# The last batch of a decoder layer taken apart: maxima spread by matmuls, inner rows turned on TensorE, two products and three row halves moved to VectorE

## The chip, the cores and the metric

The kernel runs on one core of a Trainium2 chip. The metric is the time of one execution on the device in microseconds (us); lower is better.

## The reference

One decoder layer over 16 batches of 256 rows by 256 features, float32, post-norm:

```
x = layernorm(x + attention(x))            # 16 heads of 16, bias -8*|i-j|/512, softmax
x = layernorm(x + mlstm(x, ctx, ctx))      # 4 heads of 64
x = layernorm(x + ffn(x))                  # BitLinear 256 -> 1024 -> 256, SiLU gate

mlstm, per head:  a = igate - cumsum(log_sigmoid(fgate)); m = running max of a
                  D[s,t] = exp(a[t] - m[s]) for t <= s;  C = (q k^T / 8) * D
                  h = C v / (max(|sum C|, exp(-max_log_D)) + 1e-6)
                  out = norm over the 64 features of a head, times outnorm_scale
ffn:              act_quant: scale = 127/max|row|, round to integers
                  h = silu(gate) * up;  y = act_quant(h) @ ternary(w_down)^T
```

## The kernel before, in words

The 256 rows of a batch are TT = 2 tiles of 128 partitions (index t), so most tiles are [128, 2, 256]; the inner rows `h` and `hq` of the feed-forward part are [128, 2, 1024]. Each engine has one written-out order of calls: `opening()` for the first batches, `body(b)` for batches 4 to 11 and `closing()` for the rest. The engines meet only at semaphores, and each executes its list strictly in order. Batches are overlapped: while the 16 heads of attention of batch b are computed, the mLSTM part of b-1 and the feed-forward part of b-2 run between them, so after the last attention head of batch 15 there remain its mLSTM part, the feed-forward parts of batches 14 and 15 and little else.

PSUM has eight banks: two for scores (`pS`), two for transposed scores (`pT`), one for attention outputs (`pO`), and three (`pA`, `pB`, `pC`) that all other products lease in the order in which TensorE's list asks for them. A lease waits until the product three leases back has been read.

The steps that matter here, for batch c (mLSTM) or f (feed-forward):

- Layer norms 0, 1 and 2 share one scheme. VectorE takes statistics (`row_stats`, L2786; `row_moments`, L2795) and adds epsilon (`row_eps`, L2805); GpSimd raises to the power -1/2 (`rstd`, L1411); VectorE makes the shift (`row_shift`, L2816), which waits for GpSimd; ScalarE writes both row tiles for norms 0 and 1 (`normed`, L1994), GpSimd for norm 2 (`output`, L1477).
- The gates of the mLSTM part: ScalarE reads them (L1931 to L1955), VectorE sums (`forget_sums`, L3034), GpSimd adds (`input_rows`, L1498), VectorE takes the running maximum `mm` [4, 256] (`running_max`, L3042). SyncE writes `mm` to DRAM (`save_max`, L1246) and reads it back into all 128 partitions (`spread_max`, L1253). ScalarE then exponentiates `mb` (`mem_late`, L1914; `mem_weights`, L1922), GpSimd zeroes the causal part (`mem_causal`, L1506), VectorE multiplies with the scores (`mem_weights`, L3023).
- Head norm: VectorE up to L2908 (`head_norm`), GpSimd multiplies by the norm weights (`mem_scaled`, L1514) and adds the residual (`mem_residual`, L1522), then norm 1.
- Feed-forward: rows rounded (`quantised` L2005, `quantised_rows` L1454), turned (`rows_turned` L275, `rows_copy` L2022), gate and up products in four parts (L395, L410), tanh (L2086), `gated` (L2958), `gated_up` (L2969), row maximum (`inner_max`, L2977), scale factors (L2985 to L3002), rounding on ScalarE (`scaled`, L2094) and GpSimd (`inner_quantised`, L1466), a DMA transpose per tile (`turn_inner`, L1264), the down product (`down`, L457), `ffn_residual` (L3013), norm 2 and `store` (L1269).

The PSUM banks and the few lines that cannot be told otherwise:

```
other, n = leases[-len(shared)]          # three leases back
signal, k = freed[other]
eng.wait_ge(signal.sem, signal.at(n, k))
```

Of the kernel before, what the change touches and what calls it, by code (L numbers as in the profile page):

```python
# [58 lines left out]
def build(nc, x, ctx, Wq, bq, Wk, bk, Wv, bv, Wo, bo, pos_bias, ig_w, ig_b, fg_w, fg_b, norm_w,  # L59
          w_gate, w_up, w_down, out):  # L60
    es = ExitStack()
    with es:
# [58 lines left out]
        emT = sb("emT", [P, 2, TT, XH])  # L121
        cT = sb("cT", [P, 2, 3 * P])
# [82 lines left out]
        o_out = sig("o_out", 16)  # L205

# [10 lines left out]
        leases, banks = [], {}  # L217

# [26 lines left out]

        @block.tensor
        def _(pe):
# [199 lines left out]
            def down(f, t):  # L448
# [6 lines left out]
                pe.wait_ge(hq_in[t].sem, hq_in[t].at(f, 16))  # L455
# [72 lines left out]
            def x1_turned(c, par):  # L528

                if not live(c):  # L530
                    return
                bank = lease(pe, "x1T", c)
                pe.wait_ge(x1_a.sem, x1_a.at(c, TT))
                transposes(bank, x1[:, par, :, :], ident[:], x1T_ps)

# [322 lines left out]
            def closing():  # L858
                turned(11, 15)
                mem_values(10, 0)  # L860
                mem_values(10, 1)
                mem_scores(10, 1)
                values(11, 3, 1)
                mem_values(10, 2)
                heads_turned(11, 0)
                heads_turned(11, 1)
                turned(12, 0)
                scores(12, 6, 0)
                scores(12, 7, 0)
                mem_values(10, 3)  # L870
                attention_turned(11)
                scores(12, 8, 0)
                turned(12, 1)
                turned(12, 2)
                out_proj(11)
                scores(12, 9, 0)
                turned(12, 3)
                ctx_turned(11)
                turned(12, 4)
                down(9, 0)  # L880
                turned(12, 5)
                scores(12, 10, 0)
                v_proj(13)
                x1_turned(11, 1)
                down(9, 1)
                gate_parts(11)
                scores(12, 11, 0)
                x_turned(14, 0)
                gate_sums(11)
                scores(12, 12, 0)  # L890
                values(12, 0, 0)
                k_proj(14)
                scores(12, 13, 0)
                scores(12, 14, 0)
                turned(12, 6)
                turned(12, 7)
                scores(12, 15, 0)
                q_proj(14)
                scores(13, 0, 1)
                rows_turned(10)  # L900
                gate_proj(10, 0)
                scores(13, 1, 1)
                turned(12, 8)
                values(12, 1, 0)
                turned(12, 9)
                turned(12, 10)
                scores(13, 2, 1)
                up_proj(10, 0)
                gate_proj(10, 1)
                exponents_turned(11)  # L910
                scores(13, 3, 1)
                up_proj(10, 1)
                turned(12, 11)
                up_proj(10, 2)
                gate_proj(10, 2)
                turned(12, 12)
                gate_proj(10, 3)
                values(12, 2, 0)
                scores(13, 4, 1)
                turned(12, 13)  # L920
                up_proj(10, 3)
                turned(12, 14)
                mem_scores(11, 0)
                turned(12, 15)
                mem_values(11, 0)
                scores(13, 5, 1)
                turned(13, 0)
                mem_scores(11, 1)
                values(12, 3, 0)
                mem_values(11, 1)  # L930
                scores(13, 6, 1)
                heads_turned(12, 0)
                scores(13, 7, 1)
                heads_turned(12, 1)
                mem_values(11, 2)
                turned(13, 1)
# [3 lines left out]
                out_proj(12)  # L940
                turned(13, 2)
                ctx_turned(12)
                scores(13, 9, 1)
                turned(13, 3)
                turned(13, 4)
                turned(13, 5)
                down(10, 0)
                v_proj(14)
                scores(13, 10, 1)
# [3 lines left out]
                x_turned(15, 1)  # L953
                scores(13, 11, 1)
                gate_sums(12)
                scores(13, 12, 1)
                turned(13, 6)
                values(13, 0, 1)
                scores(13, 13, 1)
                scores(13, 14, 1)  # L960
                q_proj(15)
                turned(13, 7)
                turned(13, 8)
                scores(13, 15, 1)
                k_proj(15)
                scores(14, 0, 0)
                rows_turned(11)
# [3001 lines left out]
```

## Time and profile before

| | us |
|---|---|
| median of 3 executions | 722.99 (721.27 to 723.14) |
| the profiled execution | 722.18 |
| its span, first to last instruction | 720.5 |

| engine | busy us | share of the span |
|---|---|---|
| TensorE (PE) | 622.3 | 86% |
| VectorE (DVE) | 602.0 | 84% |
| ScalarE (ACT) | 566.9 | 79% |
| GpSimd (POOL) | 505.9 | 70% |

The busy shares are averages over the whole execution; the closing part of it is much emptier than the middle. In a row of a timeline stand the start, the duration, the engine, the line, the operation, the tiles written and read with their shapes, and in brackets how long the engine had been idle and which instruction released it. Consecutive instructions of one line are merged (x2, x8).

### The profile page before, as it was taken

The numbers are of one execution on the slowest core, as the hardware profiler recorded it, in microseconds if no ns is written. First come the engines' busy times: TensorE is split into PE (matmuls) and PEld (weight loads), VectorE is DVE, ScalarE is ACT, GpSimd is POOL, SyncE is SP. The second block draws the span as 40 slices with busy tenths as digits, with TensorE's granted clock in tenths as the row PEclk, the third lists the DMA queues.
The fourth block names the chain that finished last, engine by engine and source line by source line (L and its number), as shares of the span: only waits on it lengthen the run. The fifth ranks groups of instructions, "written<-read, shape, count | busy, mean of one in ns | idle before, by whom it ended". The sixth has DMA issues, their size and how long they took to land. (4 is left out here: it accounts for less than half of the span.)

```text
span 720.5 us, 16641 instructions
## 1 busy us (share of the span) xinstructions
PE 622.3 (86%) x4892; PEld 451.7 (63%) x4892; DVE 602.0 (84%) x2387; ACT 566.9 (79%) x1189; POOL 505.9 (70%) x781
## 2 busy tenths in 40 slices
PE   5688998999999999999999999998988978684642
PEld 3465785777767676867686868676665746452311
DVE  2475798999999999999999999998979998685853
ACT  1165979899998989898989898988769687875531
POOL 3185678778897878888888888875968746644432
PEclk9599999999999999999999999999999999898856
DMA  8995939455556575647273737454194611111201
GB/s 237 142 214 119 131 76 137 98 89 123 85 104 103 104 105 101 106 93 114 78 113 83 115 66 132 70 100 79 57 131 82 115 42 46 21 61 37 73 16 44
DMA packets 106104, 69.20 MB, mean 96 GB/s; under 512 B 47200, under 2 KB 106016, under 8 KB 106016
## 3 DMA queue, kind: packets, MB, share of 16 engines
q1 hardware_dynamic: 106016, 68.14, 51.9%
q8 instruction: 41, 0.67, 0.4%
q14 instruction: 47, 0.39, 0.2%
HBM read 28.73 MB, written 4.26 MB: 46 GB/s over the span
## 5 line engine op out<-in xcount | busy, mean ns | idle before, releaser
L2774 DVE CUSTOM_DVE_ANT_0 sc<-pS,bias 128x256 f32<-128x256 f32 x512 | 198.5, 415 | 25.6 <-PE pS L291 18.4
L1444 POOL TENSOR_SCALAR sc<-sc,mx 128x256 f32<-128x256 f32 x336 | 166.5, 506 | 28.1 <-DVE mx L2774 27.0
L1895 ACT ACTIVATE pr<-pT 128x512 f32<-128x512 f32 x256 | 152.2, 614 | 16.4 <-PE pT L309 16.1
L309 PE MATMUL pT<-ident,sc 128*128 128x128 f32 x1024 | 152.9, 276 | 6.8 <-POOL sc L1444 3.8
L309 PEld LDWEIGHTS pT<-ident,sc 128*128 128x128 f32 x1024 | 118.0, 141 | 29.7 <-issue 14.7
L291 PE MATMUL pS<-ks,qs 96*128 96x256 bf16 x512 | 94.0, 275 | 7.8 <-DVE mx L2774 6.8
L1883 ACT ACTIVATE sc<-sc,mx 128x256 f32<-128x256 f32 x176 | 90.8, 528 | 3.5 <-DVE mx L2774 3.5
L291 PEld LDWEIGHTS pS<-ks,qs 96*128 96x128 bf16 x512 | 44.2, 98 | 42.6 <-DVE mx L2774 23.0
L326 PE MATMUL pO<-pr,va 128*32 128x256 f32 x1024 | 68.7, 386 | 0.6 <-ACT oT L1905 0.6
L1411 POOL TENSOR_TENSOR rs<-ve,minus_half 128x2 f32<-128x2 f32 x48 | 37.6, 782 | 33.1 <-DVE ve L2805 33.0
L1466 POOL TENSOR_SCALAR hq<-h 128x512 bf16<-128x512 f32 x64 | 38.5, 618 | 29.0 <-ACT h L2094 27.7
L1994 ACT ACTIVATE x<-y,shift,rs 128x256 f32<-128x256 f32 x64 | 34.9, 594 | 27.9 <-DVE shift L2816 27.6
L1506 POOL TENSOR_SCALAR_AFFINE_SELECT mb<-mb 128x256 f32<-128x256 f32 x64 | 26.0, 408 | 33.8 <-ACT mb L1922 33.6
L2094 ACT ACTIVATE h<-h,magic,hs 128x1024 f32<-128x1024 f32 x32 | 39.6, 1238 | 7.6 <-DVE hs L3002 7.6
L326 PEld LDWEIGHTS pO<-pr,va 128*32 128x32 f32 x1024 | 26.8, 109 | 26.5 <-issue 10.8
L2774 DVE DVE_READ_ACCUMULATOR2_ANT mx<- 128x1 f32 x512 | 41.6, 81 | 0.0
L2786 DVE BATCH_NORM_STATS2 st<-y 128x6 f32<-128x256 f32 x96 | 35.8, 416 | 5.8 <-POOL y L1522 4.3
L2977 DVE TENSOR_REDUCE hs<-h 128x1 f32<-128x1024 f32 x32 | 38.8, 1213 | 0.3
L1422 POOL TENSOR_SCALAR parts<-qk_f 128x512 bf16<-128x512 f32 x31 | 19.5, 629 | 27.7 <-ACT qk_f L2053 27.2
L1424 POOL TENSOR_TENSOR qk_f<-qk_f,parts 128x512 f32<-128x512 f32 x31 | 36.8, 1188 | 2.6
L1434 POOL TENSOR_TENSOR parts<-qk_f,parts 128x512 bf16<-128x512 f32 x31 | 36.1, 1163 | 2.6
L1922 ACT ACTIVATE mb<-mb,aT 128x256 f32<-128x256 f32 x64 | 34.6, 541 | 0.8
(291 smaller groups left out, 1672.9 us busy)
## 6 DMA issues: line engine op xcount, KB each, us to landing
qs<-parts SPq DMA_DIRECT2D x96, 128.0 KB, 4.7
ks<-parts SPq DMA_DIRECT2D x96, 128.0 KB, 4.9
mb<-mrows SPq DMA_DIRECT2D x16, 512.0 KB, 3.8
xin<-in_x SPq DMA_DIRECT2D x16, 256.0 KB, 3.6
xb<-in_x SPq DMA_DIRECT2D x16, 256.0 KB, 5.3
cx<-in_ctx SPq DMA_DIRECT2D x32, 128.0 KB, 2.1
out<-hq SPq DMA_DIRECT2D x16, 256.0 KB, 2.2
bias<-in_L_attn_pos_bias SPq DMA_DIRECT2D x4, 768.0 KB, 9.2
```

The costliest lines, as they stand in the source:

```text
L291: ins = pe.matmul(pS[s % 2][:, t * S:t * S + S], qs[par][:, s, t * P:t * P + P], ks[par][:, s, :], start=True, stop=True)
L309: ins = pe.transpose(bank[:, kt * S + t * P:kt * S + t * P + P], sc[:, s % RING, t, kt * P:kt * P + P], ident[:])
L326: ins = pe.matmul(pO[32 * j:32 * j + 32, 0:S], va[par][:, kt, hd, :], pr[:, hd % RING, kt, :], start=(kt == 0), stop=(kt == TT - 1))
L1411: pool.tensor_tensor(rs[:, which, :], ve[:, which, :], minus_half[:, 0:TT], ALU.pow)\
L1424: pool.tensor_tensor(src, src, parts[:, 0, which, :, :], ALU.subtract).then_inc(split.sem, 1)
L1444: ins = pool.tensor_scalar(sc[:, s % RING, t, :], sc[:, s % RING, t, :], -1.0, mx[:, s % RING, t:t + 1], ALU.mult, ALU.add)
L1466: ins = pool.tensor_scalar(hq[:, t, j * 512:j * 512 + 512], h[:, t, j * 512:j * 512 + 512], 1.0, -MAGIC, ALU.mult, ALU.add)
L1883: act.activation(sc[:, s % RING, 0, :], sc[:, s % RING, 0, :], ACT.Identity, bias=mx[:, s % RING, 0:1], scale=-1.0).then_inc(neg_a.sem, 1)
L1895: act.activation(flat(pr[:, s % RING, :, :]), pT[s % 2][:, :], ACT.Exp, scale=-1.0)\
L2094: act.activation(h[:, t, :], h[:, t, :], ACT.Identity, bias=magic[:, :], scale=hs[:, 4, t:t + 1])\
L2774: dve.tensor_tensor_reduce(out=sc[:, s % RING, t, :], in0=pS[s % 2][:, t * S:t * S + S], in1=bias[:, s, t * P:t * P + S][:, ::-1], scale=1 ...
L2977: dve.tensor_reduce(hs[:, 0, t:t + 1], h[:, t, :], AX.X, ALU.max, apply_absolute_value=True)\
```

## The change

`max_rows_of` makes the last batch read the running maxima from PSUM; `final(batch)` is true for batch 15 alone. For that batch:

- `save_max`, `spread_max` and both `turn_inner` leave SyncE's list. TensorE spreads the maxima by four float32 products with a selector `heads_of` (made once, in VectorE's closing list) into the score banks, and turns the inner rows by sixteen bf16 transposes into the score banks; ScalarE and VectorE copy a half each into `hqT`.
- `mem_scaled` and `mem_residual` move from GpSimd to VectorE.
- In norms 0, 1 and 2 ScalarE (or GpSimd) writes row tile 0 and VectorE row tile 1.
- ScalarE rounds the inner rows in halves of 512 columns, and GpSimd follows half by half.
- All five `closing()` lists are written anew, from batch 12 of attention on; opening and body are the same.

```diff
+        def final(batch):
+            return isinstance(batch, int) and batch == B - 1
+        def max_rows_of(c, hh):
+            return pS[hh // 2][:, hh % 2 * S:hh % 2 * S + S] if final(c) else mb[:, hh, 0:S]
...
# TensorE, down
-                pe.wait_ge(hq_in[t].sem, hq_in[t].at(f, 16))
+                if final(f):
+                    pe.wait_ge(it_a.sem, t + 1)
+                    pe.wait_ge(it_v.sem, t + 1)
+                else:
+                    pe.wait_ge(hq_in[t].sem, hq_in[t].at(f, 16))
...
+            def max_spread(c):
+                pe.wait_ge(mm_v.sem, mm_v.at(c, 1))
+                pe.wait_ge(h_of.sem, 1)
+                pe.wait_ge(s_mx.sem, TT * NH * B)
+                for hh in range(XH):
+                    ins = pe.matmul(pS[hh // 2][:, hh % 2 * S:hh % 2 * S + S], heads_of[:, hh, :], mm[:, :], start=True, stop=True)
+                ins.then_inc(spread.sem, 1)
+
+            def inner_turned(f, t):
+                pe.wait_ge(hq_g.sem, hq_g.at(f, t + 1))
+                pe.wait_ge(d_sb.sem, d_sb.at(f, 2 * XH))
+                for j in range(FT):
+                    bank = (pS, pT)[j // 4][t][:, :].bitcast(BF16)
+                    ins = pe.transpose(bank[:, j % 4 * P:j % 4 * P + P], hq[:, t, j * P:j * P + P], ident_b[:])
+                    if j % 4 == 3:
+                        ins.then_inc(it_ps.sem, 1)
...
# ScalarE, and below it VectorE
+            def inner_copy(f, t):
+                act.wait_ge(it_ps.sem, 2 * t + 1)
+                act.wait_ge(h_v.sem, h_v.at(f, 7))
+                act.activation(flat(hqT[:, t, 0:4, :]), pS[t][:, :].bitcast(BF16)[:, 0:512], ACT.Copy).then_inc(it_a.sem, 1)
...
+                n = 2 if final(f) else 1
+                for j in range(n):
+                    part = h[:, t, j * FI // n:(j + 1) * FI // n]
+                    act.activation(part, part, ACT.Identity, bias=magic[:, :], scale=hs[:, 4, t:t + 1]).then_inc(hr_a.sem, 1)
...
+            def normed_half(batch, which, par):
+                o, y = ((x1[:, par, :, :], y1), (x2, y2))[which]
+                wait(dve, rs_s[which], batch, TT)
+                if which == 1:
+                    wait(dve, y_v, batch - 1, TT)
+                dve.tensor_scalar(o[:, 1, :], y[:, 1, :], rs[:, which, 1:2], shift[:, which, 1:2], ALU.mult, ALU.add)\
+                    .then_inc(half_v[which].sem, 1)
+            def mem_scaled(f):
+                dve.wait_ge(gn_v.sem, gn_v.at(f, 16))
+                dve.tensor_tensor(y2[:], y2[:], nw_bc[:, :].unsqueeze(1).to_broadcast([P, TT, D]), ALU.mult)\
+                    .then_inc(mem_v.sem, 1)
+            def mem_residual(f, par):
+                dve.wait_ge(mem_v.sem, 1)
+                dve.tensor_tensor(y2[:], y2[:], x1[:, par, :, :], ALU.add).then_inc(mem_v.sem, 1)
+            def inner_copy(f, t):
+                dve.wait_ge(it_ps.sem, 2 * t + 2)
+                dve.wait_ge(h_v.sem, h_v.at(f, 7))
+                dve.tensor_copy(hqT[:, t, 4:8, :].rearrange("p j q -> p (j q)"), pT[t][:, :].bitcast(BF16)[:, 0:512]).then_inc(it_v.sem, 1)
+            def output_half(e):
+                wait(dve, rs_s[2], e, TT)
+                wait(dve, o_out, e - 1, 16)
+                dve.tensor_scalar(ot[:, 1, :], y3[:, 1, :], rs[:, 2, 1:2], shift[:, 2, 1:2], ALU.mult, ALU.add)\
+                    .then_inc(out_v.sem, 1)
```

The end of VectorE's new list, with what moved marked (from the last attention output on):

```diff
                 row_shift(15, 0)
+                normed_half(15, 0, 1)
                 ffn_residual(13, 0)
-                ffn_residual(13, 1)
                 row_stats(14, 1)
                 row_moments(14, 1)
+                ffn_residual(13, 1)
                 row_eps(14, 1)
                 row_shift(14, 1)
...
-                row_eps(13, 2)
                 forget_sums(15)
                 running_max(15)
                 max_rows(15)
                 gated(14, 0)
                 gated_up(14, 0)
                 gated(14, 1)
+                gated_up(14, 1)
+                row_eps(13, 2)
                 row_shift(13, 2)
-                gated_up(14, 1)
                 inner_max(14, 0)
...
                 head_norm(15)
-                ffn_residual(14, 0)
+                mem_scaled(15)
+                mem_residual(15, 1)
                 row_stats(15, 1)
                 row_moments(15, 1)
                 row_eps(15, 1)
+                ffn_residual(14, 0)
                 ffn_residual(14, 1)
                 row_shift(15, 1)
-                row_stats(14, 2)
+                normed_half(15, 1, 1)
                 row_max(15)
...
                 inner_factor(15, 1)
+                inner_copy(15, 0)
+                inner_copy(15, 1)
                 ffn_residual(15, 0)
...
                 row_shift(15, 2)
+                output_half(15)
```

And of TensorE's:

```diff
                 down(13, 0)
-                down(13, 1)
                 ctx_turned(15)
                 x1_turned(15, 1)
+                down(13, 1)
                 gate_parts(15)
...
                 gate_proj(14, 2)
+                up_proj(14, 2)
                 gate_proj(14, 3)
-                up_proj(14, 2)
+                max_spread(15)
                 up_proj(14, 3)
                 mem_scores(15, 0)
...
                 gate_proj(15, 0)
+                up_proj(15, 0)
                 gate_proj(15, 1)
-                up_proj(15, 0)
+                gate_proj(15, 2)
                 up_proj(15, 1)
-                gate_proj(15, 2)
                 gate_proj(15, 3)
                 up_proj(15, 2)
                 up_proj(15, 3)
+                inner_turned(15, 0)
+                inner_turned(15, 1)
                 down(15, 0)
                 down(15, 1)
```

On ScalarE `scaled(14, 0)` stands behind `mem_out(15, 0)` instead of ahead of `mem_weights(15, 2)`.

## Rows read from the trace of the kernel before

**Rows 1.** Busy time in three stretches (PE, PEld, DVE, ACT, POOL busy us; clock; DMA).

```profile
400.00:500.00 100.00, 96.27 (x783) 72.62 (x776) 93.33 (x398) 89.20 (x186) 80.17 (x122) 1.00 0.54 93
560.00:600.00 40.00, 32.78 (x276) 23.02 (x275) 37.18 (x146) 32.05 (x67) 25.10 (x41) 1.00 0.35 71
...
700.00:721.00 21.00, 5.81 (x24) 2.60 (x22) 8.50 (x25) 3.74 (x4) 4.20 (x7) 0.66 0.20 50
```

**Rows 2.** The chain that ended last: start, us, what ended it.

```profile
684.50 1.26 POOL y L1514
685.84 1.26 POOL y L1522
...
706.12 1.25 ACT h L2094
707.44 1.20 POOL hq L1466 x2
```

**Rows 3.** VectorE's timeline, 683 to 700 us.

```profile
683.73 0.69 DVE L2908 TENSOR_TENSOR y<-y,nrm 128x512 f32<-128x512 f32 x1 [1.53 <-POOL nrm L1486]
...
687.13 0.75 DVE L2786 BATCH_NORM_STATS2 st<-y 128x6 f32<-128x256 f32 x2 [2.32 <-POOL y L1522]
...
688.33 0.48 DVE L3013 SCALAR_TENSOR_TENSOR y<-pC,hs,x 128x256 f32<-128x256 f32 x1
...
690.74 0.69 DVE L2915 TENSOR_REDUCE fs<-x 128x2 f32<-128x512 f32 x1 [0.50 <-ACT x L1994]
...
699.50 0.69 DVE L2969 TENSOR_TENSOR h<-h,pB 128x512 f32<-128x512 f32 x1
```

**Rows 4.** ScalarE's timeline, 671 to 695 us.

```profile
671.85 0.40 ACT L1914 ACTIVATE mb<-mb,aT 128x128 f32<-128x128 f32 x1 [0.23 <-DMA mb<-mrows]
...
689.61 1.09 ACT L1994 ACTIVATE x<-y,shift,rs 128x256 f32<-128x256 f32 x2 [9.81 <-DVE shift L2816]
...
694.61 0.60 ACT L2022 ACTIVATE xqT<-pA 128x512 bf16<-128x512 bf16 x1 [1.47 <-PE pA L275]
```

**Rows 5.** VectorE's timeline, 657 to 675 us.

```profile
657.36 0.21 DVE L2805 TENSOR_SCALAR ve<-mv 128x1 f32<-128x1 f32 x2
658.39 0.33 DVE L2816 TENSOR_SCALAR shift<-mv,rs 128x1 f32<-128x1 f32 x2 [0.82 <-POOL rs L1411]
...
670.27 1.22 DVE L2977 TENSOR_REDUCE hs<-h 128x1 f32<-128x1024 f32 x1
...
674.41 0.56 DVE L3023 SCALAR_TENSOR_TENSOR cT<-pC,mb 128x384 f32<-128x384 f32 x1
```

**Rows 6.** TensorE's timeline, 648 to 712 us.

```profile
648.50 1.97 PE L370 MATMUL pA<-woT,x1T 128*128 128x256 f32 x8 [0.78 <-ACT x1T L1975]
...
670.29 0.61 PE L395 MATMUL pC<-wg,xqT 128*128 128x512 bf16 x2
...
693.99 0.59 PE L275 MATMUL pA<-ident_b,xq 128*128 128x128 bf16 x4 [8.38 <-POOL xq L1454]
...
697.01 1.06 PE L410 MATMUL pA<-wu,xqT 128*128 128x512 bf16 x2
...
710.04 1.87 PE L457 MATMUL pA<-wd,th 128*128 128x256 bf16 x8 [7.35 <-DMA th<-hq]
```

**Rows 7.** SyncE's timeline: issue time of three transfers.

```profile
666.72 0.27 SPq L1246 DMA_DIRECT2D mrows<-mm  x1
...
706.85 3.05 SPq L1264 DMA_TRANSPOSE th<-hq  x2
717.94 0.38 SPq L1269 DMA_DIRECT2D out<-hq  x1
```

**Rows 8.** The timeline of all engines at the start, 15.9 to 16.4 us.

```profile
15.91 1.40 POOL L1424 TENSOR_TENSOR qk_f<-qk_f,parts 128x512 f32<-128x512 f32 x1
16.34 1.52 DVE L2708 TENSOR_TENSOR qk_f<-qk_f,parts 128x512 f32<-128x512 f32 x1
```

**Rows 9.** GpSimd's timeline, the last instructions.

```profile
716.82 1.09 POOL L1477 TENSOR_SCALAR hq<-y,rs,shift 128x256 f32<-128x256 f32 x2 [0.48 <-DVE shift L2816]
```

More of the change, by code:

```diff
@@ L205, in build @@
         o_out = sig("o_out", 16)
+        h_of, spread, it_ps, it_a, it_v, out_v = (sig(n) for n in ("h_of", "spread", "it_ps", "it_a", "it_v", "out_v"))
+        half_v, mem_v = [sig(f"half_v{i}") for i in range(2)], sig("mem_v")
         freed = {
@@ L1475, in output @@
                 wait(pool, o_out, e - 1, 16)
-                for t in range(TT):
+                for t in range(1 if final(e) else TT):
                     ins = pool.tensor_scalar(ot[:, t, :], y3[:, t, :], rs[:, 2, t:t + 1], shift[:, 2, t:t + 1],
@@ L1992, in normed @@
                     wait(act, y_v, batch - 1, TT)
-                for t in range(TT):
+                for t in range(1 if final(batch) else TT):
                     act.activation(o[:, t, :], y[:, t, :], ACT.Identity, bias=shift[:, which, t:t + 1],
@@ L2501, in closing @@
+                mem_late(12, 0)
+                gate_tanh(11, 2)
+                exponentials(13, 12)
+                negated(13, 14)
+                mem_weights(12, 0)
+                negated(13, 15)
+                mem_late(12, 1)
+                gate_tanh(11, 3)
+                exponentials(13, 13)
+                negated(14, 0)
+                negated(14, 1)
                 mem_weights(12, 1)
                 mem_late(12, 2)
+                negated(14, 3)
+                exponentials(13, 14)
@@ L2783, in row_stats @@
                 y, signal = ((y1, ln1), (y2, ln2), (y3, ln3))[which]
-                wait(dve, *((ln1, batch, 1), (gn_g, batch, 3), (y_v, batch, 2))[which])
+                wait(dve, *((ln1, batch, 1), (mem_v, 2, 0) if final(batch) else (gn_g, batch, 3), (y_v, batch, 2))[which])
                 for t in range(TT):
@@ L3688, in closing @@
+                row_moments(12, 1)
+                ffn_residual(11, 1)
                 biased(14, 9, 0)
+                row_eps(12, 1)
                 biased(14, 9, 1)
-                ffn_residual(11, 1)
-                row_stats(12, 1)
                 row_stats(11, 2)
-                row_moments(12, 1)
-                row_eps(12, 1)
+                row_shift(12, 1)
                 biased(14, 10, 0)
-                row_shift(12, 1)
                 biased(14, 10, 1)
+                row_moments(11, 2)
@@ L3733, in closing @@
-                biased(15, 3, 0)
-                gated(12, 3)
+                gated(12, 3)
+                inner_bound(12, 0)
+                gated_up(12, 3)
+                biased(15, 3, 0)
+                mem_weights(13, 0)
+                row_shift(11, 2)
+                inner_scale(12, 0)
+                mem_weights(13, 1)
+                inner_factor(12, 0)
                 biased(15, 3, 1)
-                inner_scale(12, 0)
+                head_stats(13, 0)
+                inner_max(12, 1)
```

1011 lines of the change are left out of this document (503 added, 508 removed).

## The prediction

> **What bounds the kernel now.** I read the busy time by stretches first, then the chain of waits, then each engine's timeline after 650 us. In the middle TensorE is busy 96.3 of 100 us and VectorE 93.3: nothing there is touched. From 560 to 600 us VectorE has the most work, 37.2 of 40 us, and from 700 us on no engine is busy half the time [rows 1]: a chain of dependent steps sets the pace. The reader should see in the chain that it goes through GpSimd's two passes over y, the last rounding on ScalarE and GpSimd, then the wait for a DMA transpose and two down products [rows 2, 6]. The change works on this chain, and it also writes all closing lists anew, so two questions must be kept apart: what the last batch gains, and what its neighbours pay.
>
> The sum is made on the profiled execution: 722.18 us, a span of 720.5 and 1.7 around it, 0.8 below the median of 722.99.
>
> **Norm product and residual.** On GpSimd they start at 684.50 and 685.84 and take 1.26 each; the statistics start at 687.13 [rows 2, 3]. On VectorE a product of this size with both inputs in SBUF takes 0.69 [rows 3]; two with a hand-over of 0.03 each, from the end of `head_norm` at 684.42, put the statistics at 685.9: **-1.2**. The other end is 1.52, what VectorE took for a 128x512 difference while GpSimd ran a 1.40 us one beside it [rows 8]; twice that would be 687.5, a loss of 0.4. I take 0.69, since GpSimd's own list has nothing between `head_rstd(15)` and `rstd(15, 1)`.
>
> The Trainium skill ("SBUF — State Buffer", Who interferes with whom) says that a VectorE instruction with two SBUF inputs contends with a GpSimd instruction that reads SBUF. The two rows named last agree with it. By that rule alone, with GpSimd busy, this part would lose its gain; it is the last rival below.
>
> **Row halves.** Norm 1: ScalarE writes two tiles in 1.09 from 689.61, and the row maximum starts at 690.74 [rows 3, 4]. One tile is a little over half of it, so the maximum can start at about 690.2. VectorE's half (0.48 for the 256-column `ffn_residual` [rows 3] as the upper end) is done by then: **-0.5**. Norm 0 gives nothing: see below. Output: GpSimd writes two tiles in 1.09 from 716.82 and the store goes out at 717.94 [rows 7, 9]; with one tile each it is half: **-0.5**. Each of these is between 0 (VectorE's half as late as ScalarE's second) and -0.55.
>
> **Inner rows.** ScalarE takes 1.25 for 1024 columns and GpSimd then 1.20 for two halves [rows 2]. In halves GpSimd's last 0.6 follows ScalarE's second half, which ends some 0.3 later than the single pass (a pass of 512 takes 0.60 [rows 4], twice that and overheads about 1.5): -0.3. Then, before, 1.40 us from GpSimd's end at 708.64 to the down product at 710.04 [rows 2, 6]. After: eight transposes, four taking 0.59 at the low clock [rows 6], so about 0.14 to start and 0.9 to run, and the copies of tile 0 (0.60 on ScalarE) are over meanwhile; those of tile 1 end before the first down product does. -0.3. The down products wait behind both `inner_turned`, and stay at 1.87 each: the clock is low there before (0.66 on the mean [rows 1]). Bounds: 0 if the transposes run long, -1.5 if the clock has risen for part of the down products (a 128x512 pair takes 0.61 at 2.4 GHz and 1.06 at 1.2 [rows 6]). Together **-0.6**.
>
> **Maxima by matmuls.** The DMA pair is issued from 666.72 and ScalarE starts on `mb` at 671.85: 5.1 us [rows 4, 7]. The four products have 256 float32 columns each, like the four of L370, which took 1.97 at the high clock [rows 6]. But TensorE's list has them behind `gate_proj(14, 3)`, which was issued at 670.29, so with 0.6 for it and 0.4 for the one now ahead of it they run from 671.3 to 673.2, later than the DMA landed by 1.3. `mem_late`, `mem_weights` and the selection of head 0 need 1.4 more, so VectorE's first product (674.41 before [rows 5]) is not late only because the next part but one delays it anyway: **0**. Bounds: -0.5, and +0.9 if the clock is still low (3.9 for the four).
>
> **What the new lists cost.** Three places can be read in the lists.
> `down(13, 1)` goes behind `x1_turned(15)`, and `ffn_residual(13, 1)` from before the statistics of norm 1 of batch 14 to a place just ahead of its `row_eps`. That `row_eps` is at 657.36, and its chain releases ScalarE, whose list then runs without a gap through the gates. An `ffn_residual` takes 0.48, 0.4 of it until the next starts: **+0.4**. It also buries the half of norm 0, whose product was not the last wait here.
> `row_eps(13, 2)` stood hundreds of nanoseconds ahead of everything in an idle time; now it stands directly before `row_shift(13, 2)`, between `gated_up(14, 1)` and `inner_max(14, 0)`. The shift waits for GpSimd's power: the same pair at 657.36 and 658.39 left VectorE idle for 0.82 [rows 5]. From `inner_max` at 670.27 to 674.41 [rows 5] VectorE has hardly a gap, and the rest of batch 15 hangs on it: eps 0.1 and the wait 0.8, **+0.9**. Zero is the lower end.
> The feed-forward list of batch 15 puts `up_proj(15, 0)` ahead of `gate_proj(15, 1)` and `gate_proj(15, 2)` ahead of `up_proj(15, 1)`. A pair is 0.85 at the low clock. The second tanh then comes 0.85 later, which only just meets VectorE; the second up product ends at 699.8, while its reader started at 699.50 [rows 3]: **+0.3**, between 0 and a whole pair, 0.85.
>
> **The rest of the closing lists,** batches 12 to 15 of attention, some 480 to 650 us. The same work in another order. What I can count: in VectorE's list `row_shift` follows `row_eps` at once three more times and once less, and twice the running maximum follows the forget sums with nothing between (a similar trip through GpSimd). Each is up to 0.8 of idle VectorE, 3.2 net if each is on the path, in a stretch where VectorE has 7% to spare [rows 1]; where TensorE or ScalarE is last it costs nothing. A better packing could give as much. I take **+0.6**, between -3 and +5.
>
> **Sum:** -1.2 -0.5 -0.5 -0.6 +0 +0.4 +0.9 +0.3 +0.6 = **-0.6**: 721.6 for an execution like the profiled one, and 722.4 against the median of 722.99. A measurement of this kernel tells about 0.3%, 2.2 us, from no change, so this is no change.
>
> **The rivals.**
> 1. *The two waits cost nothing* (+0.4 and +0.9 hidden) and the rest is neutral: what is left is -2.8 +0.3 = -2.5, 720.5. For it: ScalarE and TensorE also have work in 656 to 675 us. Against: VectorE's rows there are contiguous.
> 2. *The new lists pack better* before 650 us, by 3: -0.6 -0.6 -3 = -4.2, 718.8. For it: TensorE is busy only 32.8 of 40 us from 560 on [rows 1]. Against: more round trips in VectorE's list.
> 3. *VectorE's in-order waits for GpSimd decide* (slower). It decides once the four net trips fall into 500 to 620 us while GpSimd has other work ahead of the power, so that in every second one the blocking of a two-input operation (1.52 for 0.69, 0.8 more [rows 8]) comes on top of the 0.8: four trips at 1.2 are +4.8 instead of +0.6, in all -1.2 +4.8 = +3.6, 726.6. For it: VectorE at 93% there. Against: the trips are spread over batches with slack on TensorE's side.
> 4. *GpSimd is reading SBUF while VectorE does the moved products*: +0.4 instead of -1.2, in all +1.0, 724.0. Against: its rounding of batch 14 has to end before `head_rstd(15)`.
>
> **How the numbers follow.** Forecast 0.48 (all of it within 0.3%, 720.8 to 725.2), rival 1 0.18 (three quarters of it just beyond 0.3% faster), rival 2 0.14 (faster), rival 3 0.14 (slower), rival 4 0.06 (same, a fifth slower with drift). Faster 0.13 + 0.14 = 0.27; slower 0.14 + 0.04 for the upper edge of the forecast's unknown part = 0.18; within 0.3% 0.55. Range 719.2 to 725.6: it takes in rivals 1 and 4 and part of rivals 2 and 3. The likeliest one's own range is 721.0 to 724.5.
>
> **What would show it.** VectorE's statistics of norm 1 of batch 15 start 1.5 after `head_norm(15)` ends (2.7 before), with 0.69 for each product; the row maximum starts 0.6 after the shift; `down(15, 0)` starts 1.1 after GpSimd's last half; the store is issued 0.6 after GpSimd starts its tile. VectorE is idle 0.8 before `row_shift(13, 2)`. `mem_late(15, 0)` starts at the end of the spreading products and not later than 1.5 before VectorE's first product. Wrong would be: the attention residual of batch 15 (650.5 before) moved by more than 1, which is the rest of the lists; no idle time at `row_shift(13, 2)`; down products at the high clock.

## The result, and the profile after

The changed kernel takes 729.91 us (median of 7 executions, 724.63 to 731.16), the kernel before in the same session 723.14 (720.53 to 725.09). The ratio is 1.0076, 95% interval 1.0045 to 1.0106: slower, beyond the forecast range. (The two medians differ by 6.8 us; by the ratio, in which all executions count, it is 5.5. The table of runs and the sums below go by the ratios.) The profiled execution took 729.92 with a span of 728.1.

Busy time by stretches, the same three as in [rows 1], then three finer ones of the changed kernel (PE, PEld, DVE, ACT, POOL busy us; clock; DMA):

```profile
400.00:500.00 100.00, 94.29 (x776) 71.03 (x779) 92.40 (x393) 87.49 (x185) 79.36 (x119) 1.00 0.59 99
560.00:600.00 40.00, 33.06 (x265) 23.43 (x266) 34.16 (x135) 31.24 (x67) 23.83 (x37) 0.96 0.35 68
700.00:721.00 21.00, 10.76 (x49) 5.45 (x51) 11.89 (x35) 8.55 (x13) 4.83 (x8) 0.66 0.04 14
```

VectorE is busy 34.2 of 40 us from 560 on, 37.2 before. The last row is fuller mostly since the chain of the last batch stands 8 to 10 us later.

How much later, and where it came about, is read best from three marks that every kernel of this case has: VectorE's attention residuals (L3080, after the change L3161) and GpSimd's power of head norm 15 (L1486, L1522). From the starts in the profiled executions:

| us between | before | after | |
|---|---|---|---|
| residual of batch 8 to 11 | 114.1 | 115.9 | +1.8 |
| residual of 11 to 13 | 86.2 | 85.9 | -0.3 |
| residual of 13 to 15 | 80.8 | 84.0 | +3.2 |
| residual of 15 to power of head norm 15 | 31.2 | 35.9 | +4.8 |
| that power to the end | 38.8 | 36.0 | -2.8 |

Up to the residual of batch 10 the programs are the same: from that of batch 8 on each batch takes 37.6 in both, and the 1.0 by which the two executions differ there is older. So the last row, which holds all the named steps but the maxima and the half of norm 0, gained; the two rows above it lost 8.

The gain, in VectorE's timeline of the changed kernel, answering to [rows 3]:

```profile
694.19 0.69 DVE L2955 TENSOR_TENSOR y<-y,nrm 128x512 f32<-128x512 f32 x1 [1.53 <-POOL nrm L1522]
694.92 0.69 DVE L2971 TENSOR_TENSOR y<-y,nw_bc 128x512 f32<-128x512 f32 x1
695.64 0.69 DVE L2976 TENSOR_TENSOR y<-y,x 128x512 f32<-128x512 f32 x1
696.37 0.75 DVE L2833 BATCH_NORM_STATS2 st<-y 128x6 f32<-128x256 f32 x2
...
698.84 0.41 DVE L2966 TENSOR_SCALAR x<-y,rs,shift 128x256 f32<-128x256 f32 x1
699.47 0.69 DVE L2996 TENSOR_REDUCE fs<-x 128x2 f32<-128x512 f32 x1 [0.22 <-ACT x L2032]
```

The two moved operations take 0.69 each, and the statistics follow `head_norm` without the 2.32 of idle time of [rows 3]. The row maximum starts 1.00 after the shift (698.47), 1.50 before the change. The inner rows of batch 15, on ScalarE, GpSimd and TensorE, answering to [rows 2, 6], and the output half, answering to [rows 9]:

```profile
713.25 1.52 ACT L2140 ACTIVATE h<-h,magic,hs 128x512 f32<-128x512 f32 x2 [3.61 <-DVE hs L3083]
715.07 1.52 ACT L2140 ACTIVATE h<-h,magic,hs 128x512 f32<-128x512 f32 x2 [0.30 <-DVE hs L3083]
```

```profile
716.07 1.23 POOL L1502 TENSOR_SCALAR hq<-h 128x512 bf16<-128x512 f32 x2 [0.59 <-ACT h L2140]
724.89 0.68 POOL L1513 TENSOR_SCALAR hq<-y,rs,shift 128x256 f32<-128x256 f32 x1 [0.48 <-DVE shift L2863]
```

```profile
717.35 0.61 PE L564 MATMUL pS<-ident_b,hq 128*128 128x128 bf16 x4 [0.78 <-POOL hq L1502]
...
718.17 1.92 PE L470 MATMUL pA<-wd,th 128*128 128x256 bf16 x8
```

GpSimd's last half ends at 717.30 and the down product starts at 718.17, 0.87 later; with the DMA transpose it was 1.40. The loss in the tail, in TensorE's timeline after the residual of batch 15 (656.2):

```profile
660.23 0.86 PE L284 MATMUL pC<-ident,cx 128*128 128x128 f32 x4 [2.92 <-DMA cx<-in_ctx]
...
661.78 1.91 PE L470 MATMUL pB<-wd,th 128*128 128x256 bf16 x8
...
678.27 1.99 PE L556 MATMUL pS<-mm,heads_of 4*128 4x256 f32 x8
...
681.32 0.76 PE L433 MATMUL pC<-x1T,cxT 64*128 64x256 f32 x1 [0.52 <-DVE h L3039]
```

and in VectorE's, answering to [rows 5]:

```profile
663.74 0.48 DVE L3094 SCALAR_TENSOR_TENSOR y<-pB,hs,x 128x256 f32<-128x256 f32 x1 [0.71 <-PE pB L470]
...
677.85 0.33 DVE L2863 TENSOR_SCALAR shift<-mv,rs 128x1 f32<-128x1 f32 x2 [0.81 <-POOL rs L1444]
```

TensorE waits 2.92 us for the context of batch 15, whose load the new list has behind both transposes of batch 13; SyncE issues it at 655.59, 0.62 ahead of the residual; before the change it was issued 3.75 ahead, at 646.75. The granted clock is then low, 0.50 from 661 to 663, and `down(13, 1)`, now behind `x1_turned`, takes 1.91 at that level and holds up VectorE's `ffn_residual(13, 1)` for 0.71. The shift of (13, 2) waits 0.81. And the first score product of batch 15 over 256 columns takes 0.76 at the low clock; before the change it took 0.48 at the high one.

### The profile page after: what moved, and what is told of

The parts are those of the page before. It is cut to its first block, busy times and chain, and to the rows that moved or that the text cites. A ratio compares the mean times of both kernels' runs of the same rounds, so it can differ in the third digit from the quotient of the medians.

```text
span 728.1 us, 16669 instructions
## 1 busy us (share of the span) xinstructions
PE 626.0 (86%) x4886; PEld 460.2 (63%) x4916; DVE 604.8 (83%) x2395; ACT 567.1 (78%) x1191; POOL 501.6 (69%) x778
## 4 chain that ended last, share of the span: by engine, by line
PE 43%; ACT 20%; issue 13%; DVE 9%; POOL 6%; DMA 1%; POOLq 0%; SPq 0%; ACTq 0%; DVEq 0%
PE pT L318 8%; ACT pr L1929 4%; PE pS L300 4%; PE pO L335 3%; PE pC L379 3%; DVE sc L2821 2%; ACT L1929 2%; ACT th L2129 2%; PE pA L379 2%; ACT L1993 2%; PE pB L379 1%; ACT sc L1917 1%; POOL sc L1477 1%; PE pB L284 1%; PE pA L284 1%
## 5 line engine op out<-in xcount | busy, mean ns | idle before, releaser
L1477 POOL TENSOR_SCALAR sc<-sc,mx 128x256 f32<-128x256 f32 x336 | 167.0, 507 | 36.4 <-DVE mx L2821 35.4
L318 PEld LDWEIGHTS pT<-ident,sc 128*128 128x128 f32 x1024 | 119.7, 142 | 28.2 <-issue 11.0
L1444 POOL TENSOR_TENSOR rs<-ve,minus_half 128x2 f32<-128x2 f32 x48 | 36.1, 753 | 37.7 <-DVE ve L2852 37.5
L2140 ACT ACTIVATE h<-h,magic,hs 128x1024 f32<-128x1024 f32 (+1 forms) x34 | 40.1, 1185 | 7.7 <-DVE hs L3083 7.7
L3058 DVE TENSOR_REDUCE hs<-h 128x1 f32<-128x1024 f32 x32 | 38.8, 1212 | 0.2
L1467 POOL TENSOR_TENSOR parts<-qk_f,parts 128x512 bf16<-128x512 f32 x31 | 36.1, 1163 | 2.6
L1960 ACT ACTIVATE mb<-mb,aT 128x256 f32<-128x256 f32 x60 | 32.4, 539 | 0.5
```

Source lines behind the costliest of these rows:

```text
L318: ins = pe.transpose(bank[:, kt * S + t * P:kt * S + t * P + P], sc[:, s % RING, t, kt * P:kt * P + P], ident[:])
L1477: ins = pool.tensor_scalar(sc[:, s % RING, t, :], sc[:, s % RING, t, :], -1.0, mx[:, s % RING, t:t + 1], ALU.mult, ALU.add)
L2140: act.activation(part, part, ACT.Identity, bias=magic[:, :], scale=hs[:, 4, t:t + 1]).then_inc(hr_a.sem, 1)
L3058: dve.tensor_reduce(hs[:, 0, t:t + 1], h[:, t, :], AX.X, ALU.max, apply_absolute_value=True)\
```

## The experiments

Each was timed in five rounds beside the kernel before. The table has all of them; "13 to 15", "15 to power" and "to the end" are the stretches of the table above, in the profiled execution.

| run | us | ratio, interval | 13 to 15 | 15 to power | to the end |
|---|---|---|---|---|---|
| before | 722.52 to 723.14 | 1 | 80.8 | 31.2 | 38.8 |
| the change | 729.91 | 1.0076, 1.0045-1.0106 | 84.0 | 35.9 | 36.0 |
| e1 old lists, all steps | 722.01 | 0.9992, 0.9974-1.0011 | 80.1 | 33.3 | 35.8 |
| e2 new lists, no step | 731.22 | 1.0112, 1.0091-1.0133 | 84.2 | 36.1 | 39.1 |
| e3 `row_eps(13, 2)` back | 728.20 | 1.0071, 1.0044-1.0097 | 84.2 | 35.5 | 36.1 |
| e4 context, `down(13, 1)` back | 728.17 | 1.0083, 1.0064-1.0102 | 84.1 | 35.0 | 36.1 |
| e5 e1 with maxima by DMA | 719.26 | 0.9951, 0.9937-0.9964 | 82.6 | 31.2 | 35.2 |
| e6 e1, spread over 128 rows | 718.67 | 0.9951, 0.9934-0.9968 | 82.7 | 31.4 | 35.1 |
| e7 five pairs apart | 727.49 | 1.0074, 1.0049-1.0100 | 84.5 | 36.0 | 36.1 |
| e8 old front, new tail | 724.46 | 1.0022, 1.0009-1.0034 | 80.0 | 36.1 | 36.1 |
| e9 new lists from 13 on | 727.84 | 1.0071, 1.0047-1.0095 | 84.2 | 36.0 | 36.1 |
| e10 e8, tail mended | 721.58 | 0.9996, 0.9971-1.0020 | 82.1 | 34.2 | 35.9 |
| e11 change, spread 128 rows | 725.86 | 1.0053, 1.0036-1.0069 | 84.2 | 33.3 | 35.7 |
| e12 new to 13, then e6 | 720.34 | 0.9976, 0.9957-0.9994 | 81.1 | 31.4 | 35.6 |
| e13 e9, statistics later | 727.39 | 1.0056, 1.0037-1.0074 | 84.9 | 35.4 | 36.1 |
| e14 change, all mended | 723.94 | 1.0020, 1.0005-1.0035 | 85.4 | 31.7 | 35.8 |
| e15 e13 and GpSimd | 728.18 | 1.0069, 1.0050-1.0088 | 85.2 | 36.1 | 36.1 |
| e16 e13, `down(11, 1)` ahead | 730.00 | 1.0097, 1.0069-1.0125 | 86.7 | 35.3 | 36.1 |
| e17 e14, `down(11, 1)` ahead | 725.90 | 1.0040, 1.0021-1.0060 | 87.6 | 31.3 | 35.3 |

The stretches are of one execution each, and some of these lie well above the median of their kernel: that of e10 took 726.19, that of e6 722.59, that of e5 721.86.

**Steps or lists?** e1 has the lists of the kernel before with only the named steps put in, and with both `ffn_residual(14, ...)` and `row_stats(14, 2)` moved as in the change; e2 has the new lists with the old computation. The core of e1 against the kernel before, in the tail of TensorE's list:

```diff
 gate_proj(14, 3)
 up_proj(14, 2)
+max_spread(15)
 up_proj(14, 3)
 ...
+inner_turned(15, 0)
+inner_turned(15, 1)
 down(15, 0)
```

> All steps of the change for batch 15, but on the closing lists of the kernel before (the new calls put in, nothing else moved but ffn_residual(14, 0), ffn_residual(14, 1) and row_stats(14, 2) of the last norm). Theory A, the new lists are what costs: the residual of attention of batch 15 is back at 650.5 (656.2 with the change), the stretch from there to the power of the head norm of batch 15 is back at 31.2 us (35.9 with the change), and the four gains of the tail stay (-1.2, -0.5, -0.8, -0.5): -3.0 against the kernel before, about 720. 
> The kernel before with the new closing lists and none of the steps (DMA spread, DMA transposes, products on GpSimd, whole rows on ScalarE). Theory A: slower than before by the 4.7 that the lists lose before the residual of attention 15 and by 2.1 at down(13, 1) and row_eps(13, 2), about +7, 730; the stretch residual to power of batch 15 about 33.3 us. Theory B: +5 at most, since the stretch loses only its 2.1 and the front part is partly chance: 725 to 728.

Measured 722.01 and 731.22. The lists are what costs most: 1.1% without any step. But theory B held a part too, for e1 ends 3.0 earlier by its last row and has given 2.1 of it back between the residual and the power.

**Two single waits of the tail.** e3 and e4 undo one place each in the changed kernel.

```diff
+row_eps(13, 2)            # e3, VectorE
 forget_sums(15)
 ...
-row_eps(13, 2)
 row_shift(13, 2)
+load_ctx(15)              # e4, SyncE; down(13, 1) and ffn_residual(13, 1)
 turn_inner(13, 0)         # stand directly behind (13, 0) again
```

> The changed kernel with row_eps(13, 2) back ahead of forget_sums(15). VectorE no longer idles 0.8 before row_shift(13, 2): -1.0. If the low clock in the scores of batch 15 (681 to 688 us) came from that delay, another -2: 726.9. If it came from the spreading products, only -1.0: 728.9.

> The changed kernel with load_ctx(15) back ahead of turn_inner(13, 0), down(13, 1) and ffn_residual(13, 1) back behind their first halves. The context is turned 2 us earlier, TensorE does not idle 2.9 us before it, row_eps(14, 1) is 1.1 earlier after the residual: -1.1, 728.8, by both theories; if the lost clock there also set the state of the clock later, up to -3.

By the ratios neither can be told from the change (1.0071 and 1.0083 against 1.0076), and their intervals are too wide to exclude the 1.0 and 1.1 that were expected; in the profiles the stretch to the power is 0.5 and 0.9 shorter.

**The spreading products.** e5 takes them out, e6 gives them 128 rows, of which 124 are zero:

```diff
-heads_of = sb("heads_of", [XH, XH, P])
+heads_of = sb("heads_of", [P, XH, P])      # rows 4 to 127 set to 0 once
+mmz = sb("mmz", [P, S])                    # the same; rows 0 to 3 take mm of batch 15
```

> Old closing lists and all steps but the maxima by matmuls (batch 15 has the DMA pair again). Theory A (the spreading products stand in the way of the mLSTM stage: from the attention residual of batch 15 to the power of its head norm the old lists with all steps took 33.2 us, before 31.2): this kernel gives the 2.0 back and takes 720.0, so it is faster than before by 2.6. Theory B (that stretch is longer for another reason, the spread costs nothing): 722.0, as with the spread. The end of the program, from the power of head norm on, should be 3.0 shorter than before under both.

> Old closing lists and all steps; the four spreading products contract over 128 rows (124 of them zeros) instead of 4, and so do the same work in the same time with the whole array fed. Theory A2 (the cost of the spread is where it stands, behind gate_proj(14, 3) and before up_proj(14, 3)): 722.0, with the same low clock. Theory B (no cost of the spread): 722.0.

Both come to 0.9951 of before, 3 us below e1 by the ratios, with intervals that do not overlap its own. The products themselves are hardly quicker, 1.89 against 1.99. TensorE's timeline of e1, whose products have four rows:

```profile
672.73 1.99 PE L556 MATMUL pS<-mm,heads_of 4*128 4x256 f32 x8
...
678.25 0.79 PE L433 MATMUL pC<-x1T,cxT 64*128 64x256 f32 x1
```

and of e6, 128 rows:

```profile
674.94 1.89 PE L557 MATMUL pS<-mmz,heads_of 128*128 128x256 f32 x8
...
679.91 0.48 PE L434 MATMUL pC<-x1T,cxT 64*128 64x256 f32 x1
```

The busy time by stretches of 4 us, e1 and then e6 (PE, PEld, DVE, ACT, POOL; clock; DMA):

```profile
674.00:678.00 4.00, 3.15 (x20) 2.16 (x18) 3.42 (x9) 3.13 (x7) 0.82 (x2) 0.91 0.01 4
678.00:682.00 4.00, 3.83 (x23) 3.05 (x22) 2.50 (x9) 2.02 (x6) 1.99 (x4) 0.67 0.00 0
```

```profile
674.00:678.00 4.00, 3.93 (x22) 2.71 (x22) 3.96 (x10) 2.30 (x5) 0.77 (x3) 1.00 0.19 66
678.00:682.00 4.00, 3.09 (x27) 2.55 (x24) 3.58 (x11) 3.45 (x10) 1.78 (x5) 1.00 0.00 0
```

The same sequence stands around both. After the products over 4 rows the granted clock is 0.67 in the stretch in which the scores and values of batch 15 run, and a score product takes 0.79; after those over 128 rows it is 1.00 and 0.48. The stretch from the residual to the power shows it: 33.3 against 31.4, and 31.2 with the DMA. The profiles of the other kernels say the same of the clock. In all eleven with products over 4 rows it falls to the low level within 3 us behind them; in all five with 128 rows (e6, e11, e12, e14, e17) it stays high for 9 us or more. So theory A1 is confirmed, by 12 and 7 executions for the time.

**Where in the lists?** e7 draws five of VectorE's waits for GpSimd apart; e8 keeps the old lists up to the residual of batch 15, e9 up to that of batch 13; e12 is the counterpart of e9.

```diff
 row_eps(10, 1)            # e7, one of the five
-row_shift(10, 1)
 biased(12, 11, 1)
 biased(12, 12, 0)
 biased(12, 12, 1)
+row_shift(10, 1)
```

> The changed kernel, but in VectorE's list five waits for GpSimd are drawn apart again as before the change (row_shift of (10, 1), (9, 2) and (13, 1), running_max of 11 and 12 each one to four instructions later). Theory A (VectorE's in-order waits for GpSimd are what the new lists cost before 650 us): up to 0.8 each, so the attention residual of batch 15 comes 2 to 4 earlier than with the change (656.2) and the time is 726 to 728. Theory B (the loss is elsewhere: TensorE, ScalarE or GpSimd order): the residual within 1 of 656.2 and the time 729.9, at the least 729.0.

> The changed kernel with the old closing lists up to the attention residual of batch 15 (some 456 to 650 us) on every engine, and the new ones from there. Theory A (most of the loss is made before that residual, 4.7 us by the marks of one execution): residual at 650.5 to 652, time 724.0 to 725.5, so about 5 less than the change (729.9) and 2 to 3 more than the old lists with all steps (722.0). Theory B (the marks before the residual are chance of one execution and the new tail costs it all): time 728.5 to 730.

> The changed kernel with the old closing lists up to the attention residual of batch 13 (some 570 us), the new ones from there. With the old ones up to batch 15 it took 724.5, with the new ones throughout 729.9. Theory F1 (the 4 to 5 us of the front are lost before that residual, where VectorE has the adjacent waits and the marks stand at +1.5 to +3.9): 725 to 726. Theory F2 (they are lost between the residuals of 13 and 15, where the marks go from +1.5 to +4.7): 728.5 to 730.

> The counterpart: new closing lists up to the attention residual of batch 13, the old ones from there with all steps, and the spreading products over 128 rows. With the old lists throughout it took 718.7. Theory F1 (the front's loss is made before the residual of 13): 722.0 to 723.0. Theory F2 (it is made after it): 718.5 to 719.5.

e7 has the ratio of the change, 1.0074, and its residual of batch 15, at 655.58, is within 1 of 656.2, as theory B had it. Its median of 727.49 lies in theory A's range; the ratio and the mark speak for B. So these waits cost nothing that can be told from the noise, which leaves room for about 2 us. e8 takes 724.46: the front costs 1.0076 - 1.0022, 0.54% or 3.9 us, and the tail 1.0022 - 0.9992, 0.30% or 2.2. e9 is 1.0071, so nearly all of the front's loss is made after the residual of batch 13. All kernels with the new lists there take 84.0 us or more from residual 13 to 15, those with the old ones 80.0 to 82.7. e12 against e6 leaves 0.25% for the part before 13, with intervals that overlap.

**The tail.** e10 is e8 with e3 and e4 in it; e11 the change with the 128 rows of e6.

> The kernel with the old front and new tail (724.5), in whose tail the context load of batch 15, down(13, 1) and ffn_residual(13, 1) stand where they were before the change, and row_eps(13, 2) ahead of forget_sums(15); what is left new in the tail is the order of the gate and up products, of row_shift(13, 2) beside inner_max(14, 0), and of ScalarE's mem_out. With the old tail and the same steps it was 722.0. Theory T1 (the two late groups are the price of the new tail, their waits and the low clock at 676.6 to 683.5 that follows them): 722.0 to 722.5, and the clock stays high until the spreading products. Theory T2 (each of them alone repaired left the time as it was, so the rest of the order sets it): 724.0 to 724.5, with the low clock at 677 to 683.

> The changed kernel with the spreading products over 128 rows instead of 4; with the old lists this took 3 us off (722.0 to 718.7) because the granted clock stayed high through the scores and values of batch 15. 
e10, 721.58, is as fast as e1, so the two late groups are the likely price of the tail, 0.26% or 1.9 us; the intervals of e8 and e10 overlap a little. e14 below, in which these two are put back among others, supports it: it is 0.33% below e11, with intervals that do not overlap. As T1 has it, the clock of e10 is high at the spreading products, and the low stretch of e8 at 656 to 659 is gone; it is low from 677 on, right behind the products over 4 rows. e11 gains 0.23%, which its interval does not tell from nothing, and 2.6 us in its profile between residual and power (35.9 to 33.3); its clock is high from 677 to 690. So C1 is right for the stretch, though the median of 725.9 lies 0.6 below its range; the low clock at 679 to 686 of e2, which has no spreading products, shows that it can also come without them.

**Which wait in the front?** Batch 13 to 15 of the new lists has one striking row. VectorE in e9:

```profile
578.09 0.75 DVE L2833 BATCH_NORM_STATS2 st<-y 128x6 f32<-128x256 f32 x2 [2.71 <-POOL y L1558]
```

VectorE reaches `row_stats(12, 1)` 2.71 us before GpSimd's residual is done; before the change three more score steps and both feed-forward residuals of batch 11 filled that time. e13 puts them back ahead of it; e15 also takes two `negated` passes out of GpSimd's way; e16 takes `down(11, 1)` out from behind `x1_turned(13, 1)`; e14 is the changed kernel with 128 rows, the later statistics and the places of e3, e4 and e7 put back; e17 is e14 with the down product earlier too.

```diff
 v_copy(15, 1)             # e13, VectorE
-row_stats(12, 1)
-row_moments(12, 1)
 ffn_residual(11, 1)
 biased(14, 9, 0)
-row_eps(12, 1)
 biased(14, 9, 1)
+row_stats(12, 1)
+row_moments(12, 1)
+row_eps(12, 1)
 row_stats(11, 2)
```

> The kernel with the new lists from batch 13 on (727.8), in whose VectorE list the statistics of norm 1 of batch 12 stand behind ffn_residual(11, 1) and two biased score steps, as before the change, instead of ahead of them. Theory S (VectorE's in-order wait of 2.71 us for GpSimd's mem_residual there is what the new lists cost between batches 13 and 15): that wait shrinks to 1.3 or less, the residual of batch 15 comes 1.3 or more earlier, and the time is 726.0 to 726.8. Theory R (the wait only stands where another would: TensorE, ScalarE or the power for the next row_shift then ends it): the idle time moves to a later instruction and the time stays 727.2 to 728.5.

> As e13, and in GpSimd's list negated(14, 6) and (14, 7), two passes of 0.5 us, stand behind mem_residual(12, 0) instead of ahead of mem_scaled(12). Theory S: the wait at row_stats(12, 1) goes to 0.3 or less, another 0.5 to 1.0 less than e13. Theory R: the same time as e13.

> As e13 (new lists from batch 13 on, statistics of batch 12 later: 727.4), and in TensorE's list down(11, 1) ahead of ctx_turned(13) and so of x1_turned(13, 1), which waits 1.3 us for ScalarE's norm 0. VectorE's wait of 2.13 us at ffn_residual(11, 1) must go. Theory S2 (the late down product holds VectorE, and through it scores and norms of batches 12 to 14): the residual of batch 14 comes 1 to 2 earlier, time 725.4 to 726.4. Theory R (no single place): another wait takes its place, time 726.8 to 728.

> The changed kernel (729.9) with every place mended that has been named: the spreading products over 128 rows, the context load of batch 15, down(13, 1) and ffn_residual(13, 1) at their old places, row_eps(13, 2) ahead of forget_sums(15), the five pairs of VectorE drawn apart, and the statistics of batch 12 later. The rest of the new order of all five engines stays. Theory S (single waits are the cause): 720 to 722. Theory R (the order as a whole costs it, no few places): 724 to 726, that is the 725.9 of the change with 128 rows less at most 2.

> As e14 (all named places mended in the changed kernel, 723.9), with down(11, 1) earlier as well. Theory S2: 722.0 to 723.0. Theory R: 723.5 to 724.5.

What VectorE waits for at that place in e13, and then in e16:

```profile
578.12 0.48 DVE L3094 SCALAR_TENSOR_TENSOR y<-pC,hs,x 128x256 f32<-128x256 f32 x1 [2.13 <-PE pC L470]
```

```profile
578.22 0.75 DVE L2833 BATCH_NORM_STATS2 st<-y 128x6 f32<-128x256 f32 x2 [1.62 <-POOL y L1558]
...
582.66 0.42 DVE L2821 CUSTOM_DVE_ANT_0 sc<-pS,bias 128x256 f32<-128x256 f32 x1 [2.00 <-PE pS L300]
```

The 2.71 became 2.13 at the instruction ahead, and with that released, 1.62 and 2.00. The stretch from residual 13 to 15 went from 84.2 to 84.9, 85.2 and 86.7. In e14, 1.0020, the tail's losses are gone (31.7 to the power) and the front's are not (85.4): 723.9 lies at the edge of theory R's range. e17 (1.0040) is no faster, and 725.9 is above both of its theories. Theory S fell, in both forms: by the ratios e13 and e15 (1.0056, 1.0069) can't be told from e9 (1.0071), and e16 (1.0097) is no faster than either, where 725.4 to 726.4 was expected and 730.0 measured. Taking these waits out of this order freed nothing.

The residual of batch 14, between the two marks, shows why they were the wrong place to look. From the same profiled executions:

| us between residuals | 13 to 14 | 14 to 15 |
|---|---|---|
| old order there (before, e1, e5, e6, e8, e10, e12) | 40.7 to 43.5 | 39.2 to 40.1 |
| new order (the change, e2, e3, e4, e7, e9, e11) | 41.9 | 42.1 to 42.6 |
| e13, e15 | 42.7 | 42.2, 42.6 |
| e14 | 43.2 | 42.2 |
| e16 | 44.4 | 42.2 |
| e17 | 45.5 | 42.2 |

Between 13 and 14 the new order, as it was written, is not slower than the old one. Between 14 and 15 every kernel with it is, by 2 to 3 us. The row of 2.71, the two GpSimd passes and `down(11, 1)` all stand between 13 and 14: e13 to e17 made that part longer and left the other as it was. Of all the places undone, one alone stands between 14 and 15, a pair of e7. A good part of the loss there is seen at VectorE's row maximum of norm 1 of batch 13, 12.32 after the residual of batch 14 before the change and 13.41 after it:

```profile
622.70 0.69 DVE L2915 TENSOR_REDUCE fs<-x 128x2 f32<-128x512 f32 x1 [0.68 <-ACT x L1994]
```

```profile
627.57 0.69 DVE L2996 TENSOR_REDUCE fs<-x 128x2 f32<-128x512 f32 x1 [1.67 <-ACT x L2032]
```

It waits for ScalarE's norm, which stands behind the reading of batch 14's gates in ScalarE's list; that reading starts 9.4 after the residual before the change, and 10.5 in the changed kernel. No run moved the gates.

## Why the prediction was wrong

- *Norm product and residual, -1.2*: right. The statistics start 4.23 after the power of head norm, 5.45 before: -1.22, with 0.69 for each product.
- *Row halves, -0.5 and -0.5*: right. From the statistics to the row maximum 3.10 instead of 3.61; from the statistics of norm 2 to the end 5.75 instead of 6.23.
- *Inner rows, -0.6*: right, a little low. From the last factor to the down product 3.35 instead of 4.17, -0.82; the down product starts 0.87 after GpSimd's last half, forecast 1.1. The down products stayed at the low clock, 1.92.
- *FFN list of batch 15, +0.3*: +0.21 from the first gated product to the last factor.
- *Maxima by matmuls, 0, bounds -0.5 to +0.9*: wrong in size and in reason. In the old lists e1 against e5 and e6 prices them at +3.0 by the ratios, +2.1 and +1.9 in the marks; in the new lists (e11) it is 0.23%, not clear of the noise. The sum bounded only the products' place and their own duration; the duration was as forecast, 1.99. What they cost comes behind them, at the low clock of the scores and values.
- *`down(13, 1)`, +0.4*: sized by the residual's own duration alone. `row_eps(14, 1)` moved by 1.07 more than the attention residual of batch 15: the context load is moved too, in SyncE's list, and the sum left that out.
- *`row_shift(13, 2)`, +0.9*: the wait is there, 0.81, and the pair adds 1.04. Together with the term above it is most of the tail's 2.2: 1.9 by e8 against e10, 1.0022 to 0.9996. The feed-forward order of batch 15, forecast at +0.3, is in the 2.2 as well.
- *The rest of the closing lists, +0.6, between -3 and +5*: this is the step that failed most. It was priced by counting the places where `row_shift` or the running maximum follows at once, and with +0.6 taken as "the same work in another order". It measured +3.9 (e8 against the change), near the upper end of its bounds, and not at the places that were counted (e7, 1.0074). The range, 719.2 to 725.6, left out the upper end of this term's own bounds: with +5 for +0.6 the sum is 726.8. The time lies beyond this too, because the maxima went beyond their bounds and the tail's lists came to 2.2 instead of 1.6: -3.5 +3.0 +2.2 +3.9 is +5.6, 0.76% within the rounding.

Each of the four terms of that last sum is the difference of two ratios whose intervals reach 0.1 to 0.3% to either side. Since they run in a chain from before over e5, e1 and e8 to the change, they add up by construction. The named steps, without their four-row products, are worth -3.5 us (e5: 0.9951), which the sum had as -2.8. Of the change's +0.76%, -0.49 are those steps, +0.41 the four-row products, +0.30 the tail's lists and +0.54 the front's.

Rival 3 gave the right sign, and 726.6 for it, but not the cause: its round trips through the power saved nothing measurable when undone (e7, 1.0074). Rival 4 is refuted by the 0.69 of both products. The mark that I had named as wrong, the residual of batch 15 moved by more than 1, is what was seen: +5.7, 1.0 of it before the lists differ.

What stays open is why the new order costs 3.9 us by the ratios before the tail. It is shown that nearly all of it is lost behind the residual of batch 13 (e9 against e8, intervals apart), and the marks put it between those of 14 and 15. It is also shown that VectorE's adjacent waits, the statistics' wait, GpSimd's two passes and the late down product are not it alone; only one of these, a pair of e7, stands between 14 and 15. Whether it is the late gates on ScalarE, another single place there, or the order of several engines against each other was not tested. A low clock does not explain it: from residual 14 to 15 the mean granted clock is 0.96 in the change and in e4, which take 42.1 there, and 0.96 too in e1, e5, e6 and e8, which take 39.2 to 39.4.

e5 and e6 beat both kernels: old lists with the named steps, and either the DMA for the maxima or 128 rows for the products. Either is 0.5% faster than before.

## What to carry to other kernels

Where a change both alters some steps and writes the order of everything anew, price the two apart first: the old order with the new steps is one kernel. Here it took 0.8% of loss to none, and with the products' rows filled to a gain of 0.5%. A term that is read as "the same work in another order" deserves the widest range of the sum, and the stated range has to hold that term's own bounds; here its price could not be had from counting adjacent waits. Where the order costs, split the stretch by as many marks as the engine offers before an instruction is moved: here the longest wait stood one batch ahead of the loss. And before matmuls are put in the place of a DMA, look at what runs behind them on TensorE, not only at when they end.

## What the hardware showed

- Four products over 4 rows and over 128 rows take nearly the same time, 1.99 and 1.89 us for eight instructions, but the granted clock behind them differs: 0.67 against 1.00 in the 4 us from 678 (e1, e6). It fell within 3 us of the products in all eleven kernels with 4 rows, and stayed high for 9 us or more in all five with 128. The time differs by 3 us in the old lists (0.9992 against 0.9951).
- Two groups that each told nothing when put back in the changed kernel (1.0071 and 1.0083 against 1.0076) were worth 0.26% together in the kernel with the old front (1.0022 to 0.9996, intervals that just overlap). Either alone was tried only in the changed kernel, so why they did not show there is not known.
- Between residual 13 and 15 the profiled executions of the old order take 80.0, 80.1, 80.8 and 81.1 in some kernels and 82.1, 82.6 and 82.7 in others, though the instructions there are the same; the new order took 84.0 to 84.2 in the six kernels that left it as it was. The spread of the old order lies between 13 and 14 (40.7 to 41.0, or 42.1 to 43.5). Between 14 and 15 it goes with the clock: 39.2 to 39.4 where the mean granted clock is 0.96 (e1, e5, e6, e8), 40.0 to 40.1 where it is 0.91 (before, e10, e12).
